# In even halves the output projection moves ahead of the key transposes, and the four probability transposes follow each other

## The reference

```python
x = x + attention(x)          # q, k, v projections, norm and rotation of q and k, new k and v written into a paged
                              # cache, a window of 256 keys per token, softmax, values, output projection with Wo
x = x + x @ weights[subject]  # one 64x64 matrix for each batch, over the token axis
x = x + (x @ W_base.T + low_rank_chain(x))          # adapter of rank 16, chosen per batch
x = x + (x @ W.T + x @ A[idx].T @ B[idx].T * scale) # adapter of rank 16, chosen per batch
```

## Time and profile before

| | us |
|---|---|
| median of 3 runs | 443.07 |
| lowest and highest | 441.66, 443.21 |
| span of the profiled execution | 494.4 |
| PE busy in that span | 444.6 (90%) |
| DVE, POOL, ACT busy | 311.1, 268.9, 230.2 |

### The profile page before, as it was taken

One profiled execution on the slowest core, in us unless ns is written; L12 is line 12 of the kernel. 1 busy time (PEld: TensorE's weight loads), 2 busy tenths in 40 slices (PEclk: granted clock), 3 DMA queues, 4 the chain that ended last, 5 costly groups with the idle time before them and its releaser, 6 DMA issues.

```text
span 494.4 us, 9866 instructions
## 1 busy us (share of the span) xinstructions
PE 444.6 (90%) x2890; PEld 320.9 (65%) x2890; DVE 311.1 (63%) x901; ACT 230.2 (47%) x590; POOL 268.9 (54%) x241
## 2 busy tenths in 40 slices
PE   5999999996898999989799989897979898989997
PEld 2434468453666777767577767685858675767776
DVE  4988885682646666747465757565647565666543
ACT  1322113653445555646355646554445554555541
POOL 2598157487364756555546556556555556554000
PEclk9999999999799999999989999999999999999999
DMA  6396859755346544453434445353534453434111
GB/s 199 109 302 197 296 170 288 271 144 167 85 110 179 141 115 143 115 147 99 136 100 142 113 143 129 111 147 106 149 88 122 123 141 82 123 104 109 47 54 44
DMA packets 76266, 69.08 MB, mean 140 GB/s; under 512 B 50516, under 2 KB 52692, under 8 KB 76214
## 3 DMA queue, kind: packets, MB, share of 16 engines
q1 hardware_dynamic: 57248, 42.03, 28.7%
q0 software_dynamic: 15456, 22.08, 16.5%
q10 hardware_dynamic: 3510, 4.35, 2.4%
HBM read 78.39 MB, written 11.93 MB: 183 GB/s over the span
## 4 chain that ended last, share of the span: by engine, by line
PE 71%; DVE 11%; issue 9%; ACT 4%; another core or an unknown queue 3%; DMA 2%; ACTq 0%; DVEq 0%; SPq 0%
PE banks L1112 27%; PE banks L1244 8%; PE banks L1125 7%; PE banks L1279 7%; PE banks L1252 5%; PE banks L1106 5%; PE banks L1264 5%; DVE prob L974 3%; DVE x L887 2%; PE banks L1226 2%; ACT x L662 2%; PE banks L1292 2%; DMA kvb<-kvl_dram 1%; PE banks L1378 1%
## 5 line engine op out<-in xcount | busy, mean ns | idle before, releaser
L514 POOL DMA_INDIRECT windows<-kvrows_dram,idx_all x78 | 82.6, 1059 | 63.7 <-PE banks L1264 29.0
L634 ACT ACTIVATE pt_s<-banks 112x384 f32<-112x384 f32 x128 | 57.7, 498 | 96.5 <-PE banks L1252 70.9
L514 POOL DMA_INDIRECT windows<-newkv,idx_all x78 | 79.4, 1019 | 27.6 <-issue 22.4
L974 DVE CUSTOM_DVE_ANT_0 prob<-banks,mask 128x336 f32<-128x336 f32 x128 | 58.5, 505 | 52.1 <-issue 22.4
L628 ACT ACTIVATE prob<-prob,negmax 128x336 f32<-128x336 f32 x128 | 72.4, 567 | 32.3 <-DVE negmax L974 18.3
L484 POOL TENSOR_TENSOR rstd<-ms,half 128x8 f32<-128x8 f32 x24 | 45.9, 1913 | 66.4 <-DVE ms L907 46.2
L1125 PE MATMUL banks<-wkv_s,xt_s 128*128 128x512 f32 x128 | 58.7, 616 | 5.6 <-DMA xt_s<-xt_dram 5.6
L1252 PE MATMUL banks<-cst,prob 128*112 128x128 f32 x384 | 52.7, 273 | 0.2
L1264 PE MATMUL banks<-pt_s,windows 112*64 112x128 f32 x624 | 41.8, 281 | 10.6 <-ACT pt_s L634 8.7
L1112 PE MATMUL banks<-wf_hi,x 128*128 128x512 f32 x120 | 41.7, 408 | 10.5 <-DVE x L887 10.5
L1244 PE MATMUL banks<-kt_s,qt_s 64*128 64x336 f32 x256 | 47.5, 471 | 2.8 <-issue 2.8
(11 more groups left out here) (212 smaller groups left out, 825.0 us busy)
## 6 DMA issues: line engine op xcount, KB each, us to landing
usel<-utab SPq DMA_DIRECT2D x64, 128.0 KB
xt_s<-xt_dram SPq DMA_DIRECT2D x31, 256.0 KB
newkv<-kvo SPq DMA_DIRECT2D x16, 256.0 KB
stage<-xtok_dram SPq DMA_DIRECT2D x16, 256.0 KB
tsel<-ttab SPq DMA_DIRECT2D x64, 64.0 KB
out_dram<-xo ACTq DMA_DIRECT2D x15, 256.0 KB
windows<-kvrows_dram,idx_all POOLq DMA_INDIRECT x78
windows<-newkv,idx_all POOLq DMA_INDIRECT x78
```

The lines of the kernel that those rows point to most:

```text
L514: P.indirect_dma_start(kv_s[i][:, c, :], None, newkv if new else kvrows, bass.IndirectOffsetOnAxis(ap=idx_all[:, new * CH + c, b:b + 1], a ...
L634: A.activation(pt_s[g][:], tb[g % 2][0:KP, 0:CH * 128].rearrange("p (c q) -> p c q", c=CH), ACT.Copy).then_inc(S["pt_ev"], 1)
L974: V.tensor_tensor_reduce(out=prob[b % 3][:, g, :], in0=sbk[g][:, 0:WK], in1=mask[b % 2][:], scale=-1.0 / 16, scalar=3.0e38, op0=ALU.add, o ...
```

## The change

Two lines of PE's loop move up, so that O stands directly behind Q; nothing is added or taken away, and the other engines' lists are the same.

```diff
                 if k % 2 == 0:
                     if t + 1 < TILES:
                         queries(t + 1)
+                    if t >= 1:
+                        project(t - 1)
                     keys_t(n)
                     probs_t(k, 0)
                     probs_t(k, 1)
-                    if t >= 1:
-                        project(t - 1)
                     if k == 0:
                         fold(1)
                     probs_t(k, 2)
```

## The result

The changed kernel takes 454.59 us (median of 4 runs, 454.32 to 454.79) against 442.85 us before (4 runs, 441.66 to 443.21): 11.74 us more, a ratio of 1.028 with a 95% interval of 1.0258 to 1.0301. The forecast was 451.2 us, 444 to 457: the direction and the mechanism were right, the size was 3.4 us short.

The account below looks back on a forecast made before the run. PE was taken as the bound, without gaps in even halves. 14 x 0.5 + 1.7 = 8.7 us on 443.07 gives 451.8, or 450.9 scaled; a value between, 451.2 us, was taken, range 444 to 457.

Parts of the forecast that it names:

- The bound: Even halves: PE is the bound without a gap, so a pause there is paid in full unless something later returns it.
- the waits of 21.4 us: PE's waits at its two half boundaries in the first profile's steady part: Q's on DVE 10.9 us, `base`'s on `x2_lo` 10.5.
- the lateness of the copies behind Q: ACT's copies of P, read as starting up to 2.02 us behind P01 instead of 0.53, hidden by O.
- The pause: Even halves, K to S: P2 and P3 wait for ACT's copies of P0 and P1, 0.47 us, taken as 0.5, 14 times.
- the way of two signals: Signalling allowance in the wait between ACT's copies and PE, by which 0.47 us was taken as 0.5 a half.
- the new row of waits: Expected sign in PE's list of waits: P (L1252) waiting on ACT's copy of P (L634), some 6 to 8 us.
- O earlier: O directly behind Q needs `ot_lo` at Q's end; DVE finished at least 0.33 us before, so cost 0 in 14 halves.
- The last half: Last even half, without Q: K and P01 leave the shadow of O's wait for `ot_lo`, making P23 1.7 us later.
- The wait for `ot_lo`: Expected sign: O waits for `ot_lo` only in the last even half, where the wait grows to about 1.9 us.
- Given back: Rival: the pause clears late signals behind M, shrinking `base`'s wait; partly, 445 to 448, 0.10; whole or copies hidden, 0.20.
- Hidden anyway: Rival: ACT's copies are shorter in timed runs, P2 hardly waits, 444.8 us; chance 0.20 shared with a pause returned whole.
- Dearer: Rival: copies begin late also behind O (461 us), or the clock falls (463); 454.5 to 465, chance 0.14.

Follow-up runs that it names:

- e1: The kernel before, unchanged, run once more for a second profile: span 440.4 us in a run of 442.4 us.
- e2: The changed kernel with K moved ahead of O in even halves (Q, K, O, P01, P23): 451.61 us, ratio 1.022.
- e3: The changed kernel with the last three of O's 12 matmuls put between P01 and P23: 445.21 us, ratio 1.0073.
- e4: The changed kernel with P2 of the even halves transposed into a third PSUM bank, PE's matmul order unchanged: 449.06 us, ratio 1.0149.
- e7: The changed kernel with only the last one of O's 12 matmuls put between P01 and P23: 450.39 us, ratio 1.0182.
- e6: The changed kernel with the output store's issue on ACT moved behind the four copies of P: 454.95 us, ratio 1.0285.
- e5: The changed kernel with the last even half in its old order (K, P01, O, P23): 453.09 us, ratio 1.0236.
- e8: The changed kernel with K between P01 and P23 in even halves, ACT copying P0 and P1 before K's parts: 450.62 us, ratio 1.0182.

## Why the prediction was right, and where it was short

**The bound.** "A pause that is put there is paid in full": right. Two readings of the first profile belong to that execution: the waits of 21.4 us, and the lateness of the copies behind Q. In e1 the first copy of P begins 0.77 or 0.78 us behind the start of P01 in all 14 halves with Q and O, against up to 2.02. That the timed runs have less room for waits was called an argument; e1 shows it.

**The pause.** The mechanism is shown, and it is the one forecast: two banks, ACT's chain of copies, no cover (e2, e3, e4, e7). The size is the step that failed: 0.47 worked out and 0.5 taken, against 0.70 measured, in 14 halves 2.8 us. The chain after the change names the terms. P2 was put at 1.65 us behind K and the profile has it at 1.86 (257.84 against K's start at 255.98 in PE's timeline):

- 0.13 from the end of the copy (257.71) to P2's first matmul. The prediction left "the way of two signals" at 0.03 together.
- 0.07 because the first copy of P starts at 1.23 instead of 1.16. The issue of the output store does lie beside the second K copy (256.77 to 257.11, the copy 256.82 to 257.27), but it is not free, as the prediction took it to be: e6 moves it and gets 0.06 us back.
- 0.01 in the copy's length.

So P2 is 0.63 us late (1.86 against 1.23) where the prediction had 0.42. P3 adds 0.09 where it had 0.05: from P2 to S PE's timeline has 0.83 us after (257.84 to 258.67) and 0.74 before (252.52 to 253.26). Together that is 0.72, and the tile is 0.70 us longer. That the new row of waits, 6.6 us, lies in the 6 to 8 us that were forecast is luck: each wait is listed from the modelled end of the matmul in front (0.46 us instead of 0.63) and P3's part is not in it, while 14 halves cost 9.8 us.

**O earlier.** "Cost 0 in these 14 halves" failed in the first of them. O's wait there is listed with 0.55 us and costs about 0.7: O starts 3.54 us behind Q's start (124.98 against 121.44), where Q takes 2.84 (K against Q in e1: 124.70 and 121.86). In the first profile `ot_lo` was over 0.75 us ahead of Q's end in that half; in e1 it comes 0.65 behind. In the 13 others of the changed kernel it is 0.94 us or more ahead, which is more than the 0.33 that was read, so there the forecast holds.

**The last half.** 1.7 forecast, 1.93 found (e5): K and P01 at 1.23 as worked out, and the pause of 0.70 instead of 0.5. The wait for `ot_lo`, 1.9 in the forecast, is 1.86 from the place where K would have started; the row has 1.70, from the modelled end of the matmul in front.

**The sum.** 14 x 0.70 + 0.7 + 1.93 = 12.4 us. The spans differ by 12.3, but that the two agree to 0.1 is partly luck: in the changed kernel's profile the first half with an O starts 0.42 us sooner than in e1 (Q at 121.44 and 121.86), and from there to the last M the difference is 12.7. The forecast's 8.7 lacks 2.8 in the pause, 0.7 at the first O and 0.23 in the last half; the 0.6 us that it took off for a shorter execution had no ground, for ACT's copy of P has a median of 491 ns in the changed kernel's profile against 492 in the earlier trace rows.

**The rivals.** "Given back" had nothing to give back (e1). "Hidden anyway" is refuted by the new row of waits. "Dearer" is out for the changed kernel: its copies are on time, and the granted clock of its trace is 1.000 over the whole span.

The rule of the Trainium skill, "TensorE: Matmul & The Clock Gate", section "A second HAM failure mode: psum-queue depth-cycling", that cycling through banks with short idle times can make the clock fall back and forth has no support in the changed kernel: PE waits in every even half with an O, 0.41 to 0.58 us as listed, and the clock did not fall.

## What to carry to other kernels

Where two banks are handed back and forth between PE and a copying engine, count the whole loop from the first transpose to the reuse of its bank (here 1.86 us behind K, or 1.16 behind the transposes alone), and put other work between the two pairs, at least as long as that loop exceeds PE's own work in it: here 0.70 us, three of the twelve big matmuls, is enough, and the other nine may stand elsewhere. In that loop the way back to PE (0.13 us here), and anything else in the copying engine's list, a DMA issue among it, counts too. Before reading margins in a trace, compare its span with the timed runs: here a trace that was 51 us longer showed waits that the timed runs don't have, and in one half a margin that they don't have.

## What was not expected of the hardware

- The issue of a transfer in ACT's list (0.34 us long) delays the next copy by 0.06 us when it falls between two copies (e6), although it lies mostly beside the copy in front of it.
- The same wait of 1.70 us with the same busy time in front of it (1.80 of 3.50 us) was followed by a fall of the clock to 0.54 in e8, and by full clock in the changed kernel:

```profile
419.50:423.00 3.50, 1.80 (x22) 1.15 (x16) 3.25 (x14) 2.86 (x10) 0.00 (x0) 1.00 0.01 2
423.00:426.50 3.50, 3.50 (x19) 2.91 (x20) 0.58 (x2) 0.12 (x1) 0.00 (x0) 1.00 0.28 40
```

What decides between the two is not shown. The runs do show in which kernels it appears: a mean granted clock of 0.996, which fits one such fall (estimate: 3.5 us at 0.54 in 449 us take off 0.0036), stands in 6 of the 28 timed runs of the kernels in which that wait is 1.70 us (the changed one, e3, e4, e6, e7, e8), and in none of the 30 of the others (before, e1, e2, e5), which are all at 0.999 or 1.000; the first profiled execution, at 0.986, is not among them, since its own time is not on record. Only e8's trace places the fall, so that the long wait brings it about is likely but not shown.
